# A fused two-layer attention and FFN kernel: one 64x64-quarter slot for q and k, maxima split in two subtractions, and stack copies by sequence

## The reference

```python
x = x + _L0_xattn_ref(_layernorm(x), ctx_2048, ...)   # 8 heads of 8 channels, |i-j| <= 64
x = x + _L0_ffn_ref(_layernorm(x), ...)
x = x + _L1_xattn_ref(_layernorm(x), ctx_2048, ...)   # 8 heads, rotary embedding, no band
x = x + _L1_ffn_ref(_layernorm(x), ...)
```

## Time and profile before

| | |
|---|---|
| median of 3 runs | 1358.02 us (1356.0 to 1359.34) |
| the profiled execution | 1357.87 us, of which the span is 1356.1 us |
| granted TensorE clock, mean | 0.982 |
| busy in the span | PE 94%, DVE 69%, ACT 63%, POOL 52% |
| layer 0 attention | from about 32 to 500 us |
| first FFN and the way into layer 1 | about 500 to 650 us |
| layer 1 attention | about 650 to 1110 us |
| second FFN | about 1110 to 1356 us |

### The profile page before, as it was taken

How to read it: one execution, slowest core, us unless ns; L and a number is a source line. 1 busy time by engine, 2 the same in 40 slices (tenths; PEclk the granted TensorE clock), 3 DMA queues, 4 the chain that set the end, 5 groups by cost and what they waited for, 6 DMA issues and landing times.

```text
span 1356.1 us, 36204 instructions
## 1 busy us (share of the span) xinstructions
PE 1272.2 (94%) x11164; PEld 833.3 (61%) x11164; DVE 930.4 (69%) x2052; ACT 854.8 (63%) x1849; POOL 709.6 (52%) x1297
## 2 busy tenths in 40 slices
PE   6999999999999997768999999999999989999998
PEld 3666666666666665544555556666666546666665
DVE  6888888888888874649899978888888852111110
ACT  2566666666667675556788878888888772222111
POOL 4577778777777865046555645556555410100000
PEclk9999999999999998987999989999999999999999
DMA  8554454444445440024344444444444400000000
GB/s 207 119 131 110 107 114 114 105 109 113 111 109 117 91 96 7 12 63 92 86 104 106 94 88 98 100 104 108 95 100 104 102 3 1 31 16 15 15 15 31
DMA packets 90487, 113.35 MB, mean 84 GB/s; under 512 B 13971, under 2 KB 80275, under 8 KB 82739
## 3 DMA queue, kind: packets, MB, share of 16 engines
q1 hardware_dynamic: 89216, 111.25, 35.2%
q10 hardware_dynamic: 1206, 1.29, 0.3%
HBM read 18.66 MB, written 4.19 MB: 17 GB/s over the span
## 4 chain that ended last, share of the span: by engine, by line
PE 75%; DVE 10%; issue 4%; POOL 4%; DMA 3%; ACT 3%; SPq 1%; POOLq 0%; DVEq 0%; ACTq 0%
PE bank L475 14%; PE bank L435 13%; PE bank L451 12%; PE bank L696 8%; PE bank L687 8%; PE bank L433 6%; PE bank L487 3%; DVE row_max L1136 3%; PE bank L506 2%; PE bank L538 2%; PE bank L527 2%; PE bank L516 2%; DMA Ks<-Ks 1%; PE bank L549 1%; PE bank L645 1%
## 5 line engine op out<-in xcount | busy, mean ns | idle before, releaser
L1136 DVE TENSOR_REDUCE row_max<-bank 128x2 f32<-128x384 f32 (+1 forms) x1024 | 594.4, 616 | 106.8 <-PE bank L435 102.9
L732 ACT ACTIVATE probs<-bank 128x384 f32<-128x384 f32 (+1 forms) x1024 | 539.5, 542 | 173.4 <-PE bank L451 160.3
L435 PE MATMUL bank<-Ks,Qs 96*128 96x192 bf16 (+1 forms) x2048 | 372.9, 264 | 11.3 <-DMA Ks<-Ks 6.2
L451 PE MATMUL bank<-Qs,Ks 128*128 128x192 bf16 (+1 forms) x2048 | 366.4, 260 | 13.7 <-ACT probs L732 12.4
L1360 POOL TENSOR_SCALAR_AFFINE_SELECT probs<-probs 128x256 f32<-128x256 f32 (+1 forms) x512 | 259.2, 530 | 112.4 <-ACT probs L732 91.9
L435 PEld LDWEIGHTS bank<-Ks,Qs 96*128 96x128 bf16 x2048 | 185.6, 99 | 126.8 <-DVE row_max L1136 43.1
L475 PE MATMUL bank<-probs,V 128*32 128x192 f32 (+1 forms) x4096 | 248.4, 360 | 5.4 <-POOL probs L1360 3.8
L451 PEld LDWEIGHTS bank<-Qs,Ks 128*128 128x128 bf16 x2048 | 185.7, 98 | 48.2 <-ACT probs L732 34.5
L433 PE MATMUL bank<-band,ident 128*128 128x384 bf16 x512 | 168.7, 330 | 2.5 <-DMA Ks<-Ks 2.0
L475 PEld LDWEIGHTS bank<-probs,V 128*32 128x32 f32 x4096 | 107.4, 109 | 84.4 <-issue 37.8
L1297 DVE TENSOR_TENSOR X<-bank,X 128x256 f32 (+1 forms) x32 | 13.6, 424 | 185.6 <-PE bank L696 185.6
(11 more groups left out here) (118 smaller groups left out, 1670.6 us busy)
## 6 DMA issues: line engine op xcount, KB each, us to landing
Ks<-Ks SPq DMA_DIRECT2D x64, 576.0 KB
Qs<-Qs SPq DMA_DIRECT2D x128, 192.0 KB
Qs<-Qp SPq DMA_DIRECT2D x192, 64.0 KB
Ks<-Kp SPq DMA_DIRECT2D x192, 64.0 KB
X<-in_x SPq DMA_DIRECT2D x4, 1024.0 KB, 13.4
side<-in_ctx_crossed SPq DMA_DIRECT2D x32, 128.0 KB, 2.1
side<-in_ctx SPq DMA_DIRECT2D x32, 128.0 KB, 2.1
out<-X SPq DMA_DIRECT2D x8, 512.0 KB, 3.0
```

The source lines that it names most:

```text
L435: last = nc.tensor.matmul(dst[:, blk * win:(blk + 1) * win], Qs[0:SHIFT_ROW, pair[1], h, blk * P:(blk + 1) * P], Ks[0:SHIFT_ROW, pair[1], ...
L451: last = nc.tensor.matmul(dst[:, blk * win:(blk + 1) * win], Ks[:, pair[1], h, blk * P:(blk + 1) * P], Qs[:, pair[1], h, start(blk):start( ...
L732: nc.scalar.activation(probs[:, h % 8, 0:2 * win], exp_bank[h % 2][:, 0:2 * win], ACT.Exp, scale=SCALE).then_inc(s["exped"], 1)
L1136: nc.vector.tensor_reduce(row_max[:, pair[1], h, :], bank_of(pair, h)[:, 0:2 * win].rearrange("p (b k) -> p b k", b=2), AX.X, ALU.max).the ...
```

## The change

Five things change.

- `split_max` becomes two subtractions. The upper two bytes of an fp32 number are taken as its bf16 part without rounding (`upper`), and the transposition reads them in place. `row_max` now holds the maxima and both rests.
- In layer 0, `project_qk` issues q on the two diagonal quarters (bank A) and k on the two off-diagonal ones (bank B) at h=4. k therefore comes out with its sequences swapped, and layer 0's weights are no longer spread.
- In layer 0, the stack copies go by sequence: six copies of 32 KB for q and six for k. The k copies stand behind `shift_rows(r, 1)`.
- In layer 1, `project_out` is one product with the whole array.
- In layer 0 the order of the jobs changes on all engines: v at h=7, heads at h=9, back at h=12, out, mix and relu at h=14, the residual update at h=15, `mask_group(r, 2)` ahead of `gate`.

```diff
-JOBS = {
-    "A": [("q", AHEAD), ("heads", -1), ("v", 2), ("mix", -2), ("max0", 1)],
+JOBS = ({
+    "A": [("q", AHEAD), ("v", 2), ("heads", -1), ("max0", 1), ("mix", -2)],
     "B": [("max1", 0), ("k", AHEAD), ("back", -1), ("out", -1)],
-}
+}, {
+    "A": [("q", AHEAD), ("heads", -1), ("v", 2), ("max0", 1)],
+    "B": [("max1", 0), ("k", AHEAD), ("back", -1), ("out", -1)],
+})
...
+        COPIES = (2 * PARTS, PARTS)
...
+        def upper(part):
+
+            return part.bitcast(bf16)[:, 1::2]
...
                 for j in range(PARTS):
-                    dst = bass.AP(q_stack, first + j * row, [[PARTS * row, HD], [T, HPP], [1, T]])
-                    e.dma_start(dst, Qp[:, u, j, :]).then_inc(s[f"q_in{u}"], 16)
+                    if l == 0:
+                        for seq in range(2):
+                            dst = bass.AP(q_stack, first + j * row + seq * HEADS * T,
+                                          [[PARTS * row, HD], [T, HEADS], [1, T]])
+                            e.dma_start(dst, Qp[seq * CH:(seq + 1) * CH, u, j, :]).then_inc(s[f"q_in{u}"], 16)
+                    else:
+                        dst = bass.AP(q_stack, first + j * row, [[PARTS * row, HD], [T, HPP], [1, T]])
+                        e.dma_start(dst, Qp[:, u, j, :]).then_inc(s[f"q_in{u}"], 16)
+                if l:
+                    lay_out_k(pair)
...
                 shift_rows(r, 1)
+                if l == 0:
+                    lay_out_k(at(r, 2))
                 replicate(at(r, 2))
...
-                for here in (slice(0, CH), slice(CH, P)):
+                for here in (slice(0, CH), slice(CH, P)) if l == 0 else (slice(0, P),):
                     last = nc.tensor.matmul(job_bank["B"][here, 0:T], w[here, WO, here], mixed_in[here, :],
...
+            def project_qk(pair):
...
+                halves = slice(0, CH), slice(CH, P)
+                wait_apart(e, (s["xn_ready"], num(pair) + 1), (s["A_read"], job_order(l, "A", "q", pair)),
+                           (s["B_read"], job_order(l, "B", "k", pair)))
+                for here in halves:
+                    last = nc.tensor.matmul(job_bank["A"][here, 0:T], w[here, WQ, here], xn[here, pair[1], :],
                                             start=True, stop=True)
+                last.then_inc(s["A_filled"], 1)
+                for here, there in zip(halves, halves[::-1]):
+                    last = nc.tensor.matmul(job_bank["B"][there, 0:T], w[here, WK, here], xn[here, pair[1], :],
+                                            start=True, stop=True)
                 last.then_inc(s["B_filled"], 1)
...
-            wait_apart(e, (s["maxed"], num(pair) * HPP + HEADS * (half + 1)),
-                       job_wait(s, l, *(("A", "max0"), ("B", "max1"))[half], at(pair, -1), "filled"))
-            engine.tensor_scalar(parts[:, 0, :], src, 1.0, None, ALU.mult).then_inc(step, 1)
-            e.wait_ge(step, done + 1)
-            engine.tensor_tensor(rest, src, parts[:, 0, :], ALU.subtract).then_inc(step, 1)
-            wait_apart(e, (step, done + 2))
-            engine.tensor_scalar(parts[:, 1, :], rest, 1.0, None, ALU.mult).then_inc(step, 1)
-            e.wait_ge(step, done + 3)
-            engine.tensor_tensor(parts[:, 2, :], rest, parts[:, 1, :],
+            parts, step = row_max[:, pair[1], half, :, :], s[f"max_step{half}"]
+            wait_apart(e, (s["maxed"], num(pair) * HPP + HEADS * (half + 1)))
+            engine.tensor_tensor(parts[:, 1, :], parts[:, 0, :], upper(parts[:, 0, :]), ALU.subtract).then_inc(step, 1)
+            wait_apart(e, (step, num(pair) + 1))
+            engine.tensor_tensor(parts[:, 2, :], parts[:, 1, :], upper(parts[:, 1, :]),
                                  ALU.subtract).then_inc(s[f"max_parts{half}"], 1)
```

More of the change, by code:

```diff
@@ L54, in active @@
     return not isinstance(r[0], int) or 0 <= num(r, ring) < PAIRS
-JOBS = {
-    "A": [("q", AHEAD), ("heads", -1), ("v", 2), ("mix", -2), ("max0", 1)],
+JOBS = ({
+    "A": [("q", AHEAD), ("v", 2), ("heads", -1), ("max0", 1), ("mix", -2)],
     "B": [("max1", 0), ("k", AHEAD), ("back", -1), ("out", -1)],
-}
+}, {
+    "A": [("q", AHEAD), ("heads", -1), ("v", 2), ("max0", 1)],
+    "B": [("max1", 0), ("k", AHEAD), ("back", -1), ("out", -1)],
+})
 FIRST_FULL, LAST_FULL = 2, PAIRS - 1 - AHEAD
 def job_order(layer, bank, name, pair):
-    jobs = [j for j in JOBS[bank] if layer == 0 or j[0] != "mix"]
+    jobs = JOBS[layer][bank]
     place = [j[0] for j in jobs].index(name)
@@ L341, in lay_out, with lay_out_k @@
                 for j in range(PARTS):
-                    dst = bass.AP(q_stack, first + j * row, [[PARTS * row, HD], [T, HPP], [1, T]])
-                    e.dma_start(dst, Qp[:, u, j, :]).then_inc(s[f"q_in{u}"], 16)
+                    if l == 0:
[8 more added lines that the diff above has]
+                    lay_out_k(pair)
+            def lay_out_k(pair):
+                if not active(pair):
+                    return
+                u = pair[1]
                 e.wait_ge(s["k_parts"], num(pair) + 1)
                 for i in range(PARTS):
-                    e.dma_start(Ks[COPY_ROW + i * HD:COPY_ROW + (i + 1) * HD, u, :, :],
-                                Kp[:, u, i, :]).then_inc(s[f"k_in{u}"], 16)
+                    rows = slice(COPY_ROW + i * HD, COPY_ROW + (i + 1) * HD)
+                    if l == 0:
+                        for seq in range(2):
+                            e.dma_start(Ks[rows, u, seq * HEADS:(seq + 1) * HEADS, :],
+                                        Kp[(1 - seq) * CH:(2 - seq) * CH, u, i, :]).then_inc(s[f"k_in{u}"], 16)
+                    else:
+                        e.dma_start(Ks[rows, u, :, :], Kp[:, u, i, :]).then_inc(s[f"k_in{u}"], 16)
             def replicate(pair):
@@ L504, in project_out @@
                 wait_apart(e, job_wait(s, l, "B", "back", pair, "read"))
-                for here in (slice(0, CH), slice(CH, P)):
+                for here in (slice(0, CH), slice(CH, P)) if l == 0 else (slice(0, P),):
                     last = nc.tensor.matmul(job_bank["B"][here, 0:T], w[here, WO, here], mixed_in[here, :],
+                                            start=True, stop=True)
+                last.then_inc(s["B_filled"], 1)
+            def project_qk(pair):
+                if not active(pair):
+                    return
+                halves = slice(0, CH), slice(CH, P)
[3 more added lines that the diff above has]
+                    last = nc.tensor.matmul(job_bank["A"][here, 0:T], w[here, WQ, here], xn[here, pair[1], :],
+                                            start=True, stop=True)
+                last.then_inc(s["A_filled"], 1)
+                for here, there in zip(halves, halves[::-1]):
+                    last = nc.tensor.matmul(job_bank["B"][there, 0:T], w[here, WK, here], xn[here, pair[1], :],
                                             start=True, stop=True)
@@ L526, in turn_max @@
                         (s[f"max_parts{half}"], num(pair) + 1))
-                nc.tensor.transpose(max_bank[b], max_parts[:, half, :, :].rearrange("p n h -> p (n h)"),
+                nc.tensor.transpose(max_bank[b],
+                                    upper(row_max[:, pair[1], half, :, :].rearrange("p n h -> p (n h)")),
                                     ident16[:, :]).then_inc(s[f"{b}_filled"], 1)
@@ L740, in high_part @@
                 u = pair[1]
-                wait_some(e, s[f"{name}_in{u}"], pair[0] * PARTS * 16)
+                wait_some(e, s[f"{name}_in{u}"], pair[0] * COPIES[l] * 16)
                 if l == 0:
@@ L809, in iteration @@
                 for h in heads:
-                    if h == 2 and l == 0:
+                    if h == 5 and l == 0:
                         high_part("A", "q", p3, Qp, 0)
+                        high_part("B", "k", p3, Kp, 1)
                     if h == 2 and l == 1:
@@ L817, in iteration @@
                         heads_out(m1)
-                    if h == 4 and l == 0:
-                        high_part("B", "k", p3, Kp, 1)
                     if h == 5 and l == 1:
@@ L827, in iteration @@
                         high_part("B", "k", p3, Kp, 1)
-                    if h == 8:
+                    if h == 8 - (l == 0):
                         values_out(p2)
-                    if h == 10 and l == 0:
+                    if h == 14 and l == 0:
                         relu(m1)
@@ L1214, in iteration @@
                         rotate("B", "k", p3, 1, 1)
[L1215 removed]
+                    if h == 5 and l == 0:
                         rest_of("A", "q", p3, Qp, q_rest, 0)
[L1217 removed]
+                    if h == 6 and l == 0:
                         rest_of("B", "k", p3, Kp, k_rest, 1)
@@ L1480, in blocks @@
         return m.reshape(-1, P, m.shape[1]).swapaxes(0, 1).reshape(P, FFN_BLOCKS // 2, 512)
-    w0 = [spread(_bd(w).T).T if n < 2 else _bd(w) for n, w in enumerate(w0)]
+    w0 = [_bd(w) for w in w0]
```

(2 more changed lines are left out.)

54 lines of the change are left out of this document (26 added, 28 removed).

## The result

| kernel | median us | ratio to before, 95% interval |
|---|---|---|
| before | 1358.43 | |
| changed | 1380.31 (1379.65 to 1380.66, 4 runs) | 1.0163 [1.0146, 1.0181] |

A forecast was written before the change was run, and what follows sets the result against it. TensorE's own sequence was taken to bound both attention layers. Layer 0's loop plus 5, start plus 3, last four pairs minus 1 and layer 1 minus 7 made 0 against 1357.87: 1358 us, range 1341 to 1368.

The forecast's parts named there:

- at equal cost: Layer 0: back, heads, out, mix and residual update trade places without a price, each keeping its two-head distance.
- the place behind h=0: Layer 0, TensorE from h=0's scores to h=3's transposed maxima: from 2.42 to 1.85 us with q gone from there.
- 0.1 us of standstill: Layer 0, h=5 to h=7: allowance for shifted scores waiting while ScalarE rounds q and k in a row; 0.1 us.
- TensorE line: Layer 0's pair if nothing else takes over from TensorE: 0.3 us less, 15.2 us.
- the copies: Layer 0, twelve half copies on SP: stack ready at 16.6 us, cover gone, 15.7 us a pair; start plus 3 us.
- Two subtractions: Layer 0, h=0: splitting the maxima takes 0.67 us instead of 1.24, bounds 0.4 to 0.9; 0.57 less latency.
- 4.9 of traffic and 0.7 of landing: Layer 0's stack: time after the nine-fold copy's issue at 11.0 us, making the stack ready at 16.6.
- Rival 2: Layer 0: copies cost a microsecond more, stack ready at 17.6, 16.0 us a pair, 1367 us; chance 0.20.
- rival 3: Layer 0: two quarters writing one bank take turns, slot 1.1 us instead of 0.68, 1366 us; chance 0.04.
- by itself worth nothing: Split of the maxima: VectorE's 1.1 us a pair in layer 0 and GpSimd's saving in layer 1 gain 0, in TensorE's shade.
- −7 predicted: Layer 1: out as whole-array product saves 0.24 us a pair over about 29 pairs, minus 7 us.
- Rival 4: Layer 1 gains nothing because the time goes into a wait for ScalarE or VectorE, 1365 us; chance 0.06.

The follow-up runs named there:

- e3_six: Changed kernel without the second sequence's stack copies in layer 0 (six of 32 KB, scores from stale parts); 1361.88 us.
- e11_order: Changed kernel without quarters and half copies: q and k as whole-array products at h=4, six copies of 64 KB; 1373.07 us.
- e7_both: Kernel before with the two-subtraction maxima and layer 1's out as one product, layer 0's order and copies as before; 1337.25 us.
- e12_q1: e11_order with q back at h=1 (rounding and rest at h=2) and k's rounding and rest to h=4; 1349.46 us.
- e6: Changed kernel with v moved back from h=7 to h=8, behind the value group; 1380.47 us.
- e8: e3_six with v moved back from h=7 to h=8, behind the value group; 1364.00 us.
- e10_qk1: Changed kernel, all twelve copies, with the quarters of q and k at h=1 and the maxima and their copy at h=4; 1474.12 us.
- e9_six_qk1: e3_six with the quarters of q and k at h=1 and the maxima and their copy to SBUF at h=4; 1370.23 us.

## Why the prediction was wrong

**The step that failed is the order.** The prediction priced the moved jobs "at equal cost", let the place behind h=0 shrink to 1.85 us, and left "0.1 us of standstill" for ScalarE's burst; its TensorE line was 15.2 us a pair. Without waits for copies it is 15.95 (e3_six). Over 27 pairs the 0.75 is 20 us, nearly as much as the whole miss of 22; the copies, which the prediction took for the main risk, were priced at 0.5 a pair and 3 us at the start, and cost 0.39 and 6.6. Two terms were mis-sized, and they make up the 1.27 us of e11_order:

- *The maxima behind h=3*: slot 0.82 us where the sum had 0.35, and e7_both with q in the gap has 0.33. Two subtractions were priced at 0.67 (bounds 0.4 to 0.9) from rows of the old order; they take about 0.48 there (323.15 to 323.64) and 0.98 in the new order, above the bound, because GpSimd's masks hold them up. The earlier trace rows already had the sign. The rounding (L997, 0.46 us) ends at 306.56, 0.03 us behind three masks on GpSimd (304.94 to 306.53, shown below). From 130 to 450 us the same rounding takes 0.16 us at the least and 0.57 at the most. With q at h=1 the delay is hidden: e12_q1 has the same slow subtractions (0.99 on average) and a slot of 0.40.
- *v at h=7*: slot 1.24 where e12_q1 has 0.47, and where the sum had 0.1 of standstill. v takes bank A after q, so it needs ScalarE's rounding of q (behind an exponential and the copy of the heads) and then VectorE's rest. The prediction saw ScalarE's burst, and followed it to h=7's shifted scores only, not to the bank that v needs. Moving v (e6, e8) moves the wait to those shifted scores.

0.49 and 0.77 are 1.26 a pair, against 1.27 measured. The masks beside the earlier trace rows, from GpSimd's timeline of the kernel before:

```profile
304.94 1.59 POOL L1360 TENSOR_SCALAR_AFFINE_SELECT probs<-probs 128x256 f32<-128x256 f32 x3 [0.70 <-ACT probs L732]
```

**The copies**: the mechanism was right and two sizes were off. Half copies 0.68 us from start to start (0.66 predicted), nine-fold copy after 10.65 (11.0), a wait for Ks at h=0 of up to 1.6 us in one of three pairs (1.5 predicted) and a shorter one in a second, in the loop that is two pairs long. But the stack was ready after 17.1 instead of 16.6: the nine-fold copy takes 6.5 us from its issue to its landing, where the sum had 4.9 of traffic and 0.7 of landing, a term that no row showed. And the ctx load's issue grew from 0.35 to as much as 1.97 us. The start cost 6.6 us for the further copies (3 predicted, bounds 0 to 5), 9.6 in all. Rival 2, "a microsecond more", was near in its mechanism (readiness 17.1 against its 17.6), but took its 16.0 us a pair from a TensorE line that was 0.75 too short. Half copies take as long to issue as whole ones: medians of 0.61 us for both in layer 0. The rule of the Trainium skill, page "DMA: Bandwidth & Descriptors", section "Why a DMA increments its semaphore by 16 and not by 1", fits this, since by it both use eight engines; but the page has no time for the extra writes, and that they are what makes the issue long is the prediction's guess, which no run tested.

**The quarters**: right. 0.59 us against 0.68 predicted (bounds 0.55 to 0.8); q in bank A and k in bank B, each from two quarters of different rows, do not take turns, and rival 3 falls. The rule of the Trainium skill, page "TensorEngine Tiling (Array Packing)", section "Restrictions and Gotchas", that the prediction cited, does not show in these rows: the four products start within 0.02 us of each other.

**The maxima**: The savings of VectorE and GpSimd were called "by itself worth nothing", and the gain of the shorter latency was booked only together with q's removal. Alone they give 17.3 us, 0.49 a pair in layer 0, the whole wait of 10.1 us in 20 pairs that the kernel before had there; the one row quoted, 0.29 us, was below the average of 0.48.

**Layer 1**: −7 predicted, −12 measured. The 0.24 us of out are there, but pay only together with GpSimd's shorter split, which the prediction had at zero: out alone is −1.8. That "TensorE has no slack" was nearly true (49.59 of 50 us busy), and hid that GpSimd's latency stood right behind it. Rival 4 would have been right for out alone, though the engine waited for is GpSimd and not ScalarE or VectorE.

Step by step from run to run: e7_both −21.2, order +35.8, quarters −11.2, six more copies +18.4, together the 22 us of the change. These are differences of one chain of runs, so that they add up is no test.

e12_q1 has q back but is 0.41 us a pair and 5.4 us at the start behind e7_both. Its loop's part can be read from TensorE's starts, as means a pair from 130 to 450 us: 0.25 more pass from the last scores ahead of a shifted product to that product, whose weight load waits for ScalarE's exponentials (6.7 us in 20 pairs), 0.10 more behind the turn back of the heads, 0.07 more at the maxima behind h=3. At the start, the chain of e12_q1 runs through the k copies that SP issues behind the copy of the maxima:

```profile
47.62 0.75 SPq L384
48.42 0.64 SPq L363
53.51 5.79 DMA Ks<-Ks
```

e7_both's chain of that time has no copy of k in it. So the place of the k copies, which the change moved as well, is the likely cause of these 5.4 us. No run moves it alone in a kernel with six copies; this stays open, and so does why the split meets the masks in the new order: from a group's first mask to the first subtraction pass 1.75 us in e7_both and 1.13 in the changed kernel.

## What to carry to other kernels

A job that stands where an engine would wait anyway is free: before moving it away, price the wait that it covers, and follow each moved producer to every consumer of its bank, not to the nearest one. When an operation of one kind has two durations in the trace, find out what runs beside the long one before taking a mean: here it was 0.48 us a pair. Two latencies that end at the same time are worth little one by one (0.12 and 0 us a pair in layer 1) and more together (0.37), so try such edits in pairs as well as alone.

## What the hardware showed that was not expected

- A VectorE subtraction of 128x16 takes 0.17 us, or up to 0.58 if it starts during a GpSimd mask: it ends 0.02 to 0.03 us behind that mask (81 of 89 in layer 0 of the changed kernel).
- A plain 128 KB load from DRAM takes SP 0.35 us to issue with six copies of 32 KB a pair (e3_six), a median of 0.94 and up to 1.97 with twelve.
- Waits in a loop of requests compound: with the maxima's copy at h=4 and twelve copies (e10_qk1) a pair takes 19.5 us, 3.4 more than with six half copies (e9_six_qk1), part of it by a granted clock of 0.89 in the loop.
